# A rebuilt routing front, expert weights gathered with the token rows, and a half tile in another place

## The chip, the cores and the metric

One core of a Trainium2 chip runs the kernel. The metric is device time in microseconds (us) from the start to the end of one execution. PE is the matmul engine TensorE, DVE is VectorE, ACT is ScalarE, POOL is GpSimd, and SP is the engine that only issues transfers here.

## What is computed

A mixture of experts with a residual, over 4096 tokens of 256 numbers. Every token takes the two experts (of 8) with the largest gates, each expert is a three-layer network, and the results are added to the token, weighted by the gate's softmax.

```
gate = rms_w * (x * rsqrt(mean(x*x) + EPS)) @ wg_W + wg_b + (genre_embed @ gg_W + gg_b)
gate_w = softmax(gate);  topk_w, topk_i = top_k(gate_w, 2)
cw = sum(one_hot(topk_i, 8) * topk_w[..., None], axis=-2)
h1 = relu(x @ W1[e] + b1[e]);  h2 = relu(h1 @ W2[e] + b2[e]);  out_e = h2 @ W3[e] + b3[e]
x + sum over e of out_e * cw[e]
```

W1 is 256x512, W2 is 512x512 and W3 is 512x256 for each expert. Everything is float32.

## The kernel before, in words

**Tiles.** The 8192 (token, expert) pairs are sorted by expert into *slots*. A full tile is 256 slots (two halves of 128, `SUB` = 2) of one expert. What is left over of each expert goes into halves of its own: 71 halves (`MOST`) in all, so 36 tiles (`TILES`): 28 full ones, one more full one, four places (`PAIRS`) whose halves belong to different experts, and three more full ones. Three of the four places hold two halves each (*paired* tiles, steps 29 to 31), and the fourth holds one half only (the *half tile*). `TILE_AT` sets which tile stands at which step. In the kernel before the half tile is the last step, 35 (`LAST`), behind three full tiles.

**The front.** SP loads x in eight pieces and then copies x to `out` (eight transfers), since the results are added to `out` in memory. PE and DVE compute the gates, DVE picks the two experts of each token (`pick`), and PE counts them. DVE turns the counts into the order of the experts by size (`order`, signal `s_order`, for which SP waits before it loads the first weights) and into one slot number per (token, expert) pair. The slots are then inverted, from "slot of a token" to "token of a slot", by a sum of one-hot products: for each batch of 8 columns DVE makes `hot_r` (which row of a tile, 256 wide), `hot_c` (which tile, 36 wide) and `hot_q` (`hot_c` times three values: the token's number and its weight in two fp16 parts), and PE multiplies them, 16 matmuls a batch, eight batches. DVE reads the table of token numbers `tab_from` (signal `s_from`) out of the result, and later the tables `tab_to` and `tab_w` (signal `s_tab`). After batch 3 PE sums the squares of the first two experts' weights (`weight_sums`); ACT needs these to scale and split them (`weight_scales`, `high_parts`; `low_parts` on DVE), since each fp32 product is done as three fp16 ones.

On POOL, in this order: the softmax's sums, the weights' fp16 parts, the maximum over all partitions of the tokens' norms (`partition_all_reduce`), the scale of x (`s_sx`), the first expert's constants (`parameters(0)`), and only then the wait for `s_from` and the first gather.

**The steps.** For each tile i PE does `layer2(i)`, `layer1(i+1)`, `transpose_x(i+2)`, `layer3(i)`. ACT applies bias and relu (`activate`), DVE splits the result in two fp16 parts (`split`) and finishes the tile (`finish`), and ACT multiplies by the slots' weights (`weigh`, signal `s_y`). POOL's step i copies the tile's indices, gathers the rows of tile i+3 (two indirect transfers), does in steps 0, 3, 6, 9, 12, 15 and 18 (`PARAMETERS_AT`; step 0 and then each third one) the constants of one more expert, copies the constants of tile i+2 (`copy_parameters`, signal `s_prm`, for which ACT waits before it activates tile i+2's first layer), waits for `s_y` of tile i, copies the weights of tile i+2 (`cw`), and adds tile i's rows to `out` (two indirect transfers with an addition). Each engine runs its instructions in the order in which they are written, so a wait on POOL holds everything behind it. The half tile and the paired tiles have copies of their weights of their own, made by DVE (`copy_weights`).

Of the kernel before, what the change touches and what calls it, by code (L numbers as in the profile page):

```python
# [28 lines left out]
E = 8  # L29
# [12 lines left out]

MOST = (2 * N - E) // P + E
# [4 lines left out]
NAMES = FULL + 2 * PAIRS  # L48
RING = 3
# [7 lines left out]
WSCALE = float(2.0 ** 14)  # L57
# [4 lines left out]
RUNS = BATCH // RUN  # L62
# [17 lines left out]
LOWS_AT, SQUARES_AT, SUMS_AT, HIGHS_AT, PARAMETERS_AT = {0: 2, 1: 3}, {}, {}, {}, {0: 1}  # L80
# [8 lines left out]
assert max(LOWS_AT) < min(OWN_EARLY)  # L89
SUMS_BEHIND_BATCH = 3  # L90
OUT_PARTS = 8
WARM_START = 24
WARM_TILES = 96
# [11 lines left out]
def build_moe(nc, x, small_in, cond_in, weights, b3, out):  # L105
    with ExitStack() as ctx:
# [11 lines left out]
        area = sb("area", [P, J * H], F32)  # L118
# [3 lines left out]
        tab_w = sb("tab_w", [P, COLS], F32)  # L122
# [9 lines left out]
        iota_c = sb("iota_c", [P, TILES, RUN], F16)  # L132
# [25 lines left out]
        values = sb("values", [P, 3, 2 * J], F16)  # L158
# [23 lines left out]
        xg = take(RING * SUB * H).rearrange("p (s u h) -> p s u h", s=RING, u=SUB)  # L182
# [3 lines left out]
        assert at[0] == J * H  # L186
        x_sb = area[:, :].rearrange("p (j h) -> p j h", j=J)
# [7 lines left out]
        ex = take(E * J + J)  # L195
# [3 lines left out]
        floors, odd, odd_rank, half_at, later = (take(E) for _ in range(5))  # L199
        beyond = take(E * J)  # L200
        above, at_rank, weighed = (take(E * E).rearrange("p (a b) -> p a b", a=E) for _ in range(3))
# [3 lines left out]
        cand_ex = take(E * J + J)  # L205
# [4 lines left out]
        wt = take(2 * J)  # L210
        code, pad, pos_f, wsum = (take(COLS).rearrange("p (u t) -> p u t", u=SUB) for _ in range(4))
        tile16, row16 = (take(J).bitcast(F16) for _ in range(2))
        take(J)
        pairs = area[:, at[0]:at[0] + 2 * E * J]
        hot_c = take(BATCH * TILES).bitcast(F16).rearrange("p (r g c n) -> p r g c n", r=2, n=RUN, c=TILES)
        hot_r = take(BATCH * T).bitcast(F16).rearrange("p (r c n) -> p r c n", r=2, n=BATCH)
        hot_q = take(3 * BATCH * TILES).bitcast(F16).rearrange("p (r g v c n) -> p r g v c n", r=2, n=RUN, v=3, c=TILES)
        assert at[0] <= J * H

        def unread(first, n):  # L220
# [171 lines left out]
        def _(sp):  # L392
# [17 lines left out]
            for e in range(E):  # L410
# [11 lines left out]
                if e >= FRONT:  # L422
                    b3_rows(e)
# [876 lines left out]
```

## Time and profile before

| | us |
|---|---|
| median of 3 runs (lowest, highest) | 488.8 (487.81, 489.57) |
| the profiled execution's own time | 489.31 |
| its span, first to last instruction | 487.5 |
| first weights asked for by SP | 34.62 |
| `tab_from` written | 60.54 |
| first gather issued | 65.46 |
| `layer2(0)` begins | 79.01 |

The profiled execution took 1.8 us more than its span, and 0.5 us more than the median. Times in the rows are us from the span's start. PE is busy for 90% of the span, and the slices in which it is not are the first seven of forty and the last two.

### The profile page before, as it was taken

What the parts mean: (1) busy time and instruction counts of PE and PEld (TensorE: products, weight loads), DVE (VectorE), ACT (ScalarE), POOL (GpSimd) and SP (SyncE); (2) the same over time, 40 slices, a digit from 0 to 9 for tenths busy, and PEclk for the clock granted to TensorE, in tenths of its full rate; (3) what the DMA queues carried; (4) which work ended last, traced back from release to release, by engine and by line L of the source; (5) the groups of instructions that cost most, each with busy time, mean ns of one, the idle gap of its engine ahead of it and who ended that gap; (6) DMA issues with size and microseconds to landing.
All of it is one profiled execution on the core that took longest, in us unless ns stands there. A gap on an engine that the chain in (4) does not pass through costs nothing.

```text
span 487.5 us, 13260 instructions
## 1 busy us (share of the span) xinstructions
PE 438.4 (90%) x4330; PEld 393.0 (81%) x4330; DVE 312.7 (64%) x553; ACT 290.2 (60%) x607; POOL 295.8 (61%) x450
## 2 busy tenths in 40 slices
PE   6805969999999999999999999999999999999970
PEld 5504858898888888898898888888899899998860
DVE  3899753775676756657756756645556667775540
ACT  5706803767877778678678674545455555554530
POOL 5410175167777777777767777766666576565351
PEclk8955589999999999999999999999999999999996
DMA  8919416263363453332243431332232332002221
GB/s 285 393 39 364 168 45 227 85 156 55 116 155 66 110 152 67 113 49 41 45 64 120 64 57 24 55 66 46 38 52 46 52 47 46 24 24 46 26 33 19
DMA packets 18778, 44.85 MB, mean 92 GB/s; under 512 B 3963, under 2 KB 13245, under 8 KB 16541
## 3 DMA queue, kind: packets, MB, share of 16 engines
q0 software_dynamic: 13632, 17.71, 21.6%
q1 hardware_dynamic: 5008, 26.26, 14.8%
q8 instruction: 42, 0.69, 0.6%
q14 instruction: 19, 0.16, 0.1%
q10 hardware_dynamic: 77, 0.04, 0.0%
HBM read 35.60 MB, written 13.50 MB: 101 GB/s over the span
## 4 chain that ended last, share of the span: by engine, by line
PE 43%; POOL 19%; issue 14%; ACT 8%; DVE 7%; DMA 5%; POOLq 2%; DVEq 1%; SPq 0%; ACTq 0%
PE bank L1170 29%; PE bank L1204 7%; POOL out L575 6%; ACT area L721 3%; POOL area L554 2%; POOL bound L499 2%; DMA out<-area,cto 2%; DVE area L970 2%; ACT area L707 2%; ACT w_hi L675 2%; PE bank L1053 2%; ACT area L731 1%; PE bank L1126 1%; PE bank L1146 1%; DVE area L968 1%
## 5 line engine op out<-in xcount | busy, mean ns | idle before, releaser
L1170 PE MATMUL bank<-area,w_hi 128*128 128x256 f16 x1536 | 253.7, 273 | 3.4 <-DVE area L970 2.3
L1170 PE MATMUL bank<-area,w_lo 128*128 128x256 f16 x768 | 209.4, 273 | 0.0
L721 ACT ACTIVATE area<-bank,cprm 128x256 f32<-128x256 f32 (+1 forms) x264 | 132.4, 555 | 73.0 <-PE bank L1170 64.9
L1170 PEld LDWEIGHTS bank<-area,w_hi 128*128 x1536 | 149.7, 98 | 22.1 <-issue 4.9
L968 DVE CAST area<-area 128x512 f16<-128x512 f32 (+1 forms) x144 | 65.3, 453 | 131.2 <-ACT area L721 119.9
L575 POOL DMA_INDIRECT out<-area,cto x71 | 118.6, 1671 | 44.9 <-issue 26.3
L970 DVE TENSOR_TENSOR area<-area 128x512 f16<-128x512 f32 (+1 forms) x144 | 98.9, 687 | 5.0
L554 POOL DMA_INDIRECT area<-in_x,cfrom x65 | 69.5, 1070 | 38.5 <-POOL cfrom L549 27.9
L1204 PE MATMUL bank<-w_hi,area 128*128 x512 | 89.1, 273 | 1.0 <-DVE area L970 1.0
L1170 PEld LDWEIGHTS bank<-area,w_lo 128*128 x768 | 75.1, 98 | 8.7
L731 ACT ACTIVATE area<-area,cw 128x256 f32<-128x256 f32 x71 | 32.2, 499 | 74.2 <-DVE area L975 57.0
L1204 PE MATMUL bank<-w_lo,area 128*128 x256 | 69.8, 273 | 0.0
L1204 PEld LDWEIGHTS bank<-w_hi,area 128*128 128x128 f16 x512 | 50.1, 98 | 6.7 <-issue 1.2
L549 POOL COPY cto<-tab_to 128x2 int32<-128x2 int32 x36 | 33.9, 942 | 0.0
L549 POOL COPY cw<-tab_w 128x2 f32<-128x2 f32 x36 | 7.8, 218 | 41.0 <-ACT area L731 41.0
L695 ACT ACTIVATE area<-bank,small 128x512 f16<-128x512 f32 x36 | 24.9, 692 | 10.4 <-PE bank L1126 10.4
L549 POOL COPY cfrom<-tab_from 128x2 int32<-128x2 int32 x33 | 28.8, 874 | 0.0
L776 DVE SCALAR_TENSOR_TENSOR w_lo<-stage,scale,w_hi 128x1024 f16<-128x1024 f32 x20 | 24.8, 1277 | 4.6 <-POOL cprm L562 4.6
L957 DVE SCALAR_TENSOR_TENSOR area<-bank,small,area 128x512 f16<-128x512 f32 x36 | 26.8, 745 | 0.9 <-ACT area L695 0.9
L1204 PEld LDWEIGHTS bank<-w_lo,area 128*128 128x128 f16 x256 | 25.0, 98 | 2.9
L1126 PE MATMUL bank<-ident,area 128*128 128x128 f32 x142 | 22.1, 278 | 5.8 <-DMA area<-in_x,tab_from 4.8
L975 DVE SCALAR_TENSOR_TENSOR area<-bank,cprm 128x512 f32<-128x512 f32 x32 | 23.9, 746 | 4.8 <-PE bank L1204 3.9
(203 smaller groups left out, 486.5 us busy)
## 6 DMA issues: line engine op xcount, KB each, us to landing
stage<-in_weights SPq DMA_DIRECT2D x10, 1024.0 KB, 6.9
area<-in_x SPq DMA_DIRECT2D x8, 512.0 KB, 8.2
out<-in_x SPq DMA_DIRECT2D x8, 512.0 KB, 13.7
w_lo<-in_weights SPq DMA_DIRECT2D x4, 1024.0 KB
w_hi<-in_weights SPq DMA_DIRECT2D x2, 1024.0 KB, 9.9
out<-area,cto POOLq DMA_INDIRECT x71
area<-in_x,cfrom POOLq DMA_INDIRECT x65
prm<-in_b SPq DMA_DIRECT2D x8, 128.0 KB, 11.3
```

The lines of the kernel that those rows point to most:

```text
L549: pool.tensor_copy(to, table[:, bass.ds(i * SUB, SUB)]).then_inc(signal, 1)
L554: pool.indirect_dma_start(out=xg[:, s, u, :], out_offset=None, in_=x, in_offset=bass.IndirectOffsetOnAxis(ap=rows[:, u:u + 1].bitcast(U32) ...
L575: pool.indirect_dma_start(out=out, out_offset=bass.IndirectOffsetOnAxis(ap=cto[:, s, u:u + 1].bitcast(U32), axis=0), in_=yb[:, s, u, :], i ...
L695: act.activation(xt_hi, ps_x[:, :], ACT.Copy, scale=sx).then_inc(s_xhi, 1)
L721: ins = act.activation(to[:, m * T + u * wide:m * T + (u + 1) * wide], ps_h[layer][b][:, a * T + u * wide:a * T + (u + 1) * wide], ACT.Rel ...
L731: act.activation(yb[:, slot, u, :], y32[:, u * H:(u + 1) * H], ACT.Copy, scale=cw[:, slot, u:u + 1]).then_inc(s_y, 1)
L957: dve.scalar_tensor_tensor(xt_lo, ps_x[:, :], sx, xt_hi, ALU.mult, ALU.subtract).then_inc(s_xs, 1)
L968: dve.tensor_copy(hi_b, h_b).then_inc(half_done, 1)
L970: dve.tensor_tensor(lo_b, h_b, hi_b, ALU.subtract).then_inc(signal, 1)
L1126: ins = nc.tensor.transpose(ps_x[:, k * T + u * P:k * T + (u + 1) * P], xg[:, slot, u, k * P:(k + 1) * P], ident[:, :])
L1170: ins = nc.tensor.matmul(banks[m // 2][:, (m % 2) * T + u * wide:(m % 2) * T + (u + 1) * wide], weight, xp[:, cols], start=(k == 0 and n = ...
L1204: ins = nc.tensor.matmul(ps_y[:, u * H:(u + 1) * H], hp[:, cols], wp[:, bass.ds(w[u % len(w)] + (W3_AT + k * H), H)], start=(k == 0 and n ...
```

## The change

1. **Weights with the rows.** A new array in memory, `x_ext`, has for each token its 256 numbers and its 8 softmax weights (`ROW` = 264), with one spare row in the middle. SP fills the x part in the place where it copied x to `out` (rows of 1024 bytes at a pitch of 1056). POOL forms all 8 weights of each token (`dense`), and ACT issues two transfers that write them, 32 bytes to each row. The gathers read `x_ext` and wait for `s_ext`. `tab_w` is gone. POOL takes a tile's weights out of its gathered rows (`copy_weights` on POOL, behind the wait for `s_y`, with a register load of `order`).
2. **The copy of x to `out`** goes to SP's queue between the sixth and the seventh piece of weights, once the gather of tile 2 has landed. POOL waits for it (`s_out0`) before step 0, as it did before.
3. **A smaller inversion.** `hot_r` is 128 wide, `hot_c` has 72 columns and is multiplied by the token's number alone. All batches have buffers of their own. PE does 8 matmuls a batch. `tab_from` is one instruction from the result.
4. **Counts first.** The counts are summed over a partition before PE, the scan and the reciprocal run while PE counts, and instructions that don't depend on each other stand between those that do. `order` is written behind `upto` and `beyond`.
5. **The maximum over partitions** is a matmul by ones (`peaks`) in place of POOL's library function. The sums of the biases go to POOL, into its idle time.
6. **Second expert later.** ACT does `high_parts(1)` behind the second expert's squares, `(2)` behind `x_high(0)` and `(3)` in step 0. PE sums the second expert's squares behind the inversion; of the 96 warming matmuls 72 are left, 48 ahead of that sum and 24 behind it.
7. **The half tile** is step 32, directly behind the paired tiles. The last step is a full tile, whose third layer, finish, weighting and additions go by halves (`by_halves`, `layer3_parts`).

```diff
-AFTER = PAIRED_AT + PAIRS - 1
-LAST = TILES - 1
-TILE_AT = [*range(LEAST), *range(FULL - 1, LAST), *range(LEAST, FULL - 1), LAST]
+HALF_AT = PAIRED_AT + PAIRS - 1
+AFTER = HALF_AT + 1
+TILE_AT = [*range(LEAST), *range(FULL - 1, TILES), *range(LEAST, FULL - 1)]
-LOWS_AT, SQUARES_AT, SUMS_AT, HIGHS_AT, PARAMETERS_AT = {0: 2, 1: 3}, {}, {}, {}, {0: 1}
+LOWS_AT, SQUARES_AT, SUMS_AT, HIGHS_AT, PARAMETERS_AT = {0: 2, 1: 3}, {}, {}, {0: 3}, {0: 1}
...
+            sp.dma_start(x_ext[N // 2:N // 2 + 1, 0:H], x[0:1, :]).then_inc(s_ext, 16)
...
-            link(pool.partition_all_reduce(xmax_all, xmax, P, RED.max))
+            pool.tensor_tensor(je(dense), je(ex), over_e(rs), ALU.mult).then_inc(s_dense, 1)
+            pool.wait_ge(s_peak, 1)
...
+            def copy_weights(i, s, experts):
+                pool.wait_ge(s_xg[s], gathered(i) * 16)
+                for u, e in enumerate(experts):
+                    label = pool.value_load(order[0:1, bass.ds(e, 1)], min_val=0, max_val=E - 1)
+                    us = slice(u, u + 1) if paired(i) else slice(0, SUB)
+                    ins = pool.tensor_copy(cw[:, s, us].unsqueeze(2), xg[:, s, us, bass.ds(label + H, 1)])
+                ins.then_inc(s_cw, 1)
...
+            pool.wait_ge(s_ext, (OUT_PARTS + 4) * 16)
             pool.wait_ge(s_from, 1)
...
+            act.wait_ge(s_dense, 1)
+            for h in range(2):
+                first = h * (N // 2 + 1)
+                act.dma_start(x_ext[first:first + N // 2, H:ROW].rearrange("(p j) e -> p j e", j=J),
+                              je(dense)[h * P // 2:(h + 1) * P // 2]).then_inc(s_ext, 16)
...
-            inv = ps_slots.rearrange("p u (v t) -> p u v t", v=3)
-            link(dve.tensor_scalar(pos_f, inv[:, :, 0, :], 0.0, None, ALU.is_gt))
-            link(dve.scalar_tensor_tensor(code, inv[:, :, 0, :], float(N // 2), pos_f, ALU.add, ALU.subtract))
-            dve.tensor_copy(by_half(tab_from), code).then_inc(s_from, 1)
+            dve.wait_ge(s_inv, BATCHES)
+            dve.tensor_scalar(tab_from[:, :], ps_slots, float(N // 2), None, ALU.add).then_inc(s_from, 1)
```

**Place one, DVE's loop of the inversion.** Two batches of the kernel before. `iota_c` and `w_lo` hold the constants compared with, `values` the numbers multiplied in.

```order
L926 TENSOR_TENSOR area<-w_lo,area 128x2048 [waits s_spread,s_iota,s_dve]
L928 TENSOR_TENSOR area<-iota_c,area 128x288
L935 TENSOR_TENSOR area<-area,values 128x432 [waits s_wt,s_dve]
L935 TENSOR_TENSOR area<-area,values 128x432
L926 TENSOR_TENSOR area<-w_lo,area 128x2048
L928 TENSOR_TENSOR area<-iota_c,area 128x288
L935 TENSOR_TENSOR area<-area,values 128x432 [waits s_dve]
L935 TENSOR_TENSOR area<-area,values 128x432
L926 TENSOR_TENSOR area<-w_lo,area 128x2048 [waits s_inv]
```

Three batches of the kernel after; `w_hi` and `w_lo` are the buffers of their own.

```order
L985 TENSOR_TENSOR w_lo<-iota_c,area 128x1152 [waits s_spread,s_iota,s_dve]
L989 TENSOR_TENSOR w_hi<-w_lo,area 128x1024
L993 TENSOR_TENSOR w_lo<-w_lo,values 128x1152 [waits s_dve]
L989 TENSOR_TENSOR w_hi<-w_lo,area 128x1024
L985 TENSOR_TENSOR w_lo<-iota_c,area 128x1152
```

Four instructions for two batches stand in the place of eight, half as wide or less for each batch, and the wait for `s_inv` from the third batch on is gone.

**Place two, POOL's step 1.** Before, from the copy of the indices to the additions:

```order
L549 COPY cfrom<-tab_from 128x2 [waits s_xp]
L554 DMA area<-in_x,cfrom 128x256 [waits s_idx]
L554 DMA area<-in_x,cfrom 128x256
L561 TENSOR_LOAD etile
L561 ISA x2
L562 ISA
L562 COPY cprm<-prm 128x268
L549 COPY cw<-tab_w 128x2 [waits s_y,s_add]
L575 DMA out<-area,cto 4096x256 x2
```

After:

```order
L581 DMA area<-x_ext,cfrom 128x264
L589 TENSOR_LOAD etile
L589 ISA x2
L590 ISA
L590 COPY cprm<-prm 128x268
L599 ISA [waits s_y,s_add,s_xg0]
L599 TENSOR_LOAD order
L599 ISA x2
L601 ISA
L601 COPY cw<-area 128x2
L613 DMA out<-area,cto 4096x256 x2
```

Behind the wait for `s_y` there is now a register load and its arithmetic before the copy of the weights, and so before the two additions.

**Place three, SP's queue.** Before, from the load of x to the first weights, and then the seventh piece of weights:

```order
L397 DMA area<-in_x 128x1024 x7
L402 DMA out<-in_x 16x8192 x8
L411 TENSOR_LOAD order [waits s_order]
...
L417 ISA [waits s_low,s_xg1]
L417 DMA stage<-in_weights 128x2048
```

After, the same places:

```order
L415 DMA area<-in_x 128x1024 x7
L421 DMA x_ext<-in_x 512x256 x8
L422 DMA x_ext<-in_x 16x16
L423 DMA x_ext<-in_x 8x1
L432 TENSOR_LOAD order [waits s_order]
...
L438 DMA out<-in_x 16x8192 [waits s_xg2]
L438 DMA out<-in_x 16x8192 x7
L441 ISA [waits s_low]
L441 DMA stage<-in_weights 128x2048
```

The copy to `out` was in front of all weights; now one into `x_ext` in rows of 256 numbers is there, and the copy to `out` is behind the third tile's gather. The two transfers of ACT are `x_ext<-area 2048x1x8` in the same notation.

## Rows read from the trace of the kernel before

**Rows 1.** PE's waits from 80 to 450 us: engine, line, releaser, total, times, longest.
```profile
PE bank L1170 <- DVE area L970: 2.3, 5, 0.5
```

**Rows 2.** Busy time by stage: us, busy us of engines (x instructions), PE clock, DMA, GB/s.
```profile
30.00:40.00 10.00, 0.55 (x2) 0.00 (x0) 9.16 (x36) 0.97 (x2) 2.68 (x7) 0.50 0.43 164
...
60.00:70.00 10.00, 5.15 (x93) 5.01 (x90) 5.04 (x18) 1.13 (x2) 7.07 (x18) 0.99 0.09 27
```

**Rows 3.** Timeline of DVE in the front: start, us, line, operation [idle before <-releaser].
```profile
29.05 0.29 DVE L854 TENSOR_TENSOR area<-area 128x256 f16<-128x256 f16 x1
...
33.47 0.17 DVE L879 CAST order<-area 128x8 int32<-128x8 f32 x1
...
39.53 1.23 DVE L926 TENSOR_TENSOR area<-w_lo,area 128x2048 f16<-128x2048 f16 x1
40.67 0.30 DVE L928 TENSOR_TENSOR area<-iota_c,area 128x288 f16<-128x288 f16 x1
41.01 0.68 DVE L935 TENSOR_TENSOR area<-area,values 128x432 f16<-128x432 f16 x2
...
57.76 1.28 DVE L776 SCALAR_TENSOR_TENSOR w_lo<-stage,scale,w_hi 128x1024 f16<-128x1024 f32 x1
```

**Rows 4.** Timeline of ACT and of PE in the front.
```profile
41.90 1.06 ACT L656 ACTIVATE w_hi<-stage 128x1024 bf16<-128x1024 f32 x1 [0.41 <-DMA stage<-in_weights]
...
49.66 0.54 PE L1080 MATMUL bank<-small,ones 128*128 128x16 f32 x2
...
57.90 1.87 PE L1111 MATMUL bank<-area 128*128 128x108 f16 x16 [0.21 <-DVE area L935]
...
69.98 1.09 PE L1126 MATMUL bank<-ident,area 128*128 128x128 f32 x4 [4.85 <-DMA area<-in_x,tab_from]
```

**Rows 5.** Timeline of POOL and of SP's queue in the front.
```profile
47.38 0.46 POOL L538 PARTITION_ALL_REDUCE small<-small  x1 [10.23 <-issue]
57.26 0.39 POOL L539 TENSOR_SCALAR small<-small 128x1 f32<-128x1 f32 x1 [9.41 <-issue]
...
60.82 0.30 POOL L499 TENSOR_SCALAR bound<-fsq,small 128x1 f32<-128x1 f32 x1 [1.29 <-issue]
...
65.46 1.30 POOL L554 DMA_INDIRECT area<-in_x,tab_from  x1 [0.57 <-POOL prm L516]
...
73.71 0.95 POOL L554 DMA_INDIRECT area<-in_x,tab_from  x1 [0.30 <-issue]
...
34.62 1.99 SPq L417 DMA_DIRECT2D stage<-in_weights  x3
```

**Rows 6.** The chain that ended last, steps 0 and 1: start, us, what.
```profile
79.01 8.03 PE bank L1170 x72
...
90.09 7.86 PE bank L1170 x72
```

**Rows 7.** DMA queues in four windows (1.75:2, 78.5:79, 118:118.5, 16:24): packets, MB, share.
```profile
q1 hardware_dynamic: 10, 0.04, 104.4%
q10 hardware_dynamic: 52, 0.03, 42.3%
...
q1 hardware_dynamic: 16, 0.13, 66.7%
q0 software_dynamic: 15, 0.06, 29.8%
...
q0 software_dynamic: 58, 0.06, 86.7%
...
q1 hardware_dynamic: 184, 3.02, 103.7%
```

**Rows 8.** Timeline of POOL, step 3 with the constants of an expert.
```profile
114.79 0.18 POOL L549 COPY cw<-tab_w 128x2 f32<-128x2 f32 x1 [0.43 <-ACT area L731]
...
130.15 0.81 POOL L562 COPY cprm<-prm 128x268 f32 x1 [0.73 <-POOL prm L516]
```

**Rows 9.** Timeline of POOL at the end.
```profile
478.86 1.55 POOL L575 DMA_INDIRECT out<-area,cto  x1 [3.13 <-DMA out<-area,cto]
```

More of the change, by code:

```diff
@@ L198, in build_moe @@
         cmp_h = take((2 * PAIRS + 1) * E)
-        floors, odd, odd_rank, half_at, later = (take(E) for _ in range(5))
+        floors, odd, odd_rank, half_at, later, base = (take(E) for _ in range(6))
+        rowtot = take(E // 2).bitcast(F16)
         beyond = take(E * J)
-        above, at_rank, weighed = (take(E * E).rearrange("p (a b) -> p a b", a=E) for _ in range(3))
+        above, at_rank, weighed, below = (take(E * E).rearrange("p (a b) -> p a b", a=E) for _ in range(4))
         key, rank_of, order_f = (take(E) for _ in range(3))
@@ L262, in halves_of, with halves_before @@
         def halves_of(i):
-            return MOST - SUB * i if i == LAST else SUB
+            return MOST - SUB * (TILES - 1) if i == HALF_AT else SUB
+        def halves_before(i):
+            return sum(halves_of(n) for n in range(i))
         def two(i):
@@ L289, in rows, with gathered @@
             return ap.rearrange("p (e j) -> p e j", e=E)
-        def by_half(table):
-            return table[:, :].rearrange("p (t u) -> p u t", u=SUB)
+        def gathered(i):
+            return sum(halves_of(n) for n in range(i % RING, i + 1, RING))
         def over_j(ap):
@@ L413, in _ @@
                     if q == PLACES:
-                        sp.wait_ge(s_xg[1], SUB * 16)
+                        sp.wait_ge(s_xg[2], SUB * 16)
+                        for n in range(OUT_PARTS):
+                            rows = slice(n * N // OUT_PARTS, (n + 1) * N // OUT_PARTS)
+                            sp.dma_start(out[rows, :], x[rows, :]).then_inc(s_out0, 16)
                     if BEFORE[q] is not None:
@@ L886, in _ @@
-            link(dve.tensor_reduce(half_at, weighed, AX.X, ALU.add))
-            link(dve.tensor_scalar(half_at, half_at, -1.0, float(MOST * P), ALU.mult, ALU.add))
-            link(dve.tensor_tensor(later, half_at, rows_end, ALU.subtract))
+            link(dve.tensor_tensor(rows(sel16), ej(oh1), ej(oh2), ALU.add))
+            with nc.allow_low_precision(reason="counts up to J are whole numbers"):
+                dve.tensor_reduce(rowtot, rows(sel16), AX.X, ALU.add).then_inc(s_sel, 1)
+            dve.tensor_tensor_scan(running, restart[:, :], sel16, 0.0, ALU.mult, ALU.add)
@@ L999, in step @@
                 split(i, 1)
-                if next1 and two(i) and two(i + 1):
+                if next1 and two(i) and paired(i + 1):
                     copy_weights(i + 1, 0, 1)
@@ L1007, in step @@
                     x_low(i + 2)
-                if next2 and i + 2 > PAIRED_AT and two(i + 2):
-                    for u in range(SUB):
+                if next2 and i + 2 > PAIRED_AT and paired(i + 2):
+                    for u in range(halves_of(i + 2)):
                         copy_weights(i + 2, u, 0)
@@ L1234, in layer3_last, with step @@
                             ins.then_inc(s_l3, 1)
-            def step(i, s, turn, sums=None, next1=True, next2=True):
+            def step(i, s, sums=None, next1=True, next2=True):
                 w = weights_at(i)
```

357 lines of the change are left out of this document (192 added, 165 removed).

## The prediction, made before the changed kernel was run

> **What bounds the kernel now.** I read the busy times by stage first, then the timelines of the five engines up to the first steps, then PE's waits, then the DMA queues. There are three regimes. From step 0 on PE sets the pace: between 80 and 450 us its only waits of note are five of at most 0.5 us, 2.3 us together [rows 1]. The end costs a few us more. The front is the reserve: PE is busy for 0.55 of the ten us from 30 on, at a granted clock of 0.50 [rows 2].
>
> In the front two chains run to the first gather at 65.46 us. One is DVE's: the picks until 29.05, `order` at 33.47, the slots until 39.53, the loop of the inversion until 57.76, PE's last batch until 57.90 + 1.87 = 59.77 [rows 3, 4], and `tab_from` behind it. The other is POOL's. It stands before its library function for 10.23 us and behind it for 9.41, and is free only at 57.26. The constants of the first expert begin at 60.82, and the gather follows them at 65.46 [rows 5]. So the gather is issued some 5 us later than the table would allow. From the gather to `layer2(0)` at 79.01 it is 13.55 us [rows 5, 6].
>
> **The change part by part.** Against the profiled execution's 489.3 us.
>
> *Slots.* Six instructions' worth of waiting between dependent ones goes, an addition goes, and the reciprocal runs while PE counts; one reduction, one strided addition and one maximum from PSUM come, some 0.3 us each. I take the last slot at 37.8 in place of 39.5, and `order` about 1 us later (34.6), since two wide instructions now stand in front of it. So the weights land 1 us later too. Bounds: 0.5 to 2.5 us gained.
>
> *Loop.* A 2048-wide comparison takes 40.67 - 39.53 = 1.14 us to the next start, a 432-wide product 0.30 (two of them 0.68 with their latency) [rows 3]. By width, 1024 columns are 0.60 and 1152 are 0.67. A pair of batches is 2 x 0.67 + 2 x 0.60 = 2.55, four pairs are 10.2, and the loop ends at 48.0 (before 57.76). PE needs 1.87 / 16 = 0.117 us a matmul at the low clock [rows 4], 0.94 a batch, and keeps up until batch 3. There it stands before the first expert's sums. The squares of its second piece begin at 41.90 and take 2.3 [rows 4]; 1 us later they end at 45.2. The sums are three matmuls like the one of 0.54 at 49.66 [rows 4], pipelined about 1.4, so 46.6, and the last 32 matmuls 3.8: 50.4. `tab_from` is one instruction behind: 50.7, in place of 60.5.
>
> *POOL.* Without the library function POOL waits for ACT's scales, at 47.5. The constants took 65.46 - 60.82 = 4.64 with the gap in front of the gather [rows 5]: first gather at 52.3, in place of 65.46, if `x_ext` is full. That is 13.2 us sooner, and POOL is now behind the table by 1.6 only.
>
> *Gather to step 0.* Alone it would repeat. But the six pieces of weights still move until about 56, and beside such a piece POOL's and SP's queues shared a half us with 15 and 16 packets [rows 7]; I add 1.5 us to the first landing. PE gets a clock of 1.00 for the transposes and saves 0.5, and DVE, ACT have their other pieces done. `layer2(0)` begins at 66.2, which is 12.8 us sooner. Bounds: 10 to 15.
>
> *Is `x_ext` full at 52.3?* The x part, in 4096 rows, follows x on the queue; the copy it replaces moved 3.02 MB in 8 us [rows 7]. An add row, which reads and writes memory, is the dearest row of that size: 58 packets in 0.867 x 16 x 0.5 us, 0.12 us each [rows 7]. x itself is as large as the copy and goes first, until about 13.7. So the 4096 rows take between 11 and 31 us on 16 DMA engines and end between 25 and 45. I take 16 us, ready by 30, nearer the plain copy. The weights' part is 4096 pieces of 32 bytes. The reciprocal ends by 31.2, POOL's product takes 0.8 and ACT's issue and the start of a transfer 1.8: from 33.8 on. Small packets of the ACT queue went at 52 in 0.25 us beside SP's 4 KB ones, on 11 of the 16 DMA engines [rows 7]; at that rate 4096 take about 14 us, and end at 47.5. Hidden by 5 us. This is the thin cover of the whole change.
>
> *The copy to `out`.* Its gate is the third gather, whose last half was issued 73.71 - 65.46 = 8.25 us behind the first and lands some 2.7 later: 63.3. At 3.02 MB in 8 us [rows 7] the 4.19 MB take 11.1, with issue and landing 13.5: 76.8. POOL waits there with step 0 behind it. Then come the gather of tile 3 (3.6 us), the constants of the second expert (3.9) and the copy for tile 2 (1.2): 85.5. ACT wants that copy when `layer1(2)` ends: a step of 11.0 and 72 matmuls of 7.9, less a little, behind `layer2(0)` [rows 6]. That is 18.6, at 84.8, and what follows on ACT and DVE takes as long as PE has other work. I take a stall of 1.6 us; bounds 0 and 4 (POOL's lateness carried into step 3).
>
> *The register load on POOL.* In a step with constants the chain runs from `s_y` at 114.79 through POOL's additions, gather and constants to `cprm` at 130.15 + 0.81, and ACT, DVE and PE follow [rows 8]: these are the steps in which PE waits 0.5 us [rows 1]. So POOL's path has no slack there, six times. The nearest price of a load with its arithmetic is the gap of 0.73 before `cprm` [rows 8], less 0.1 for the handover that is there anyhow: 0.65 each, 3.9 us. Bounds: 0, if hidden, and 8, if the 1056-byte rows also make a gather's issue as dear as an addition's (1.55 for about 1.0).
>
> *The end.* The half tile's steps on PE are too short to cover the latency of activation and split behind `layer1`: about 1 us each at the two steps around it. At the end two rows of additions instead of one follow a longer last layer, but `layer1(35)` covers what cost 1.05 before. The last addition no longer stands 3.13 us for the one before [rows 9], since the one before is older by then. I count +0.6; bounds -1 and +2.5.
>
> *Sum.* -12.8 + 1.6 + 3.9 + 0.6 = -6.7: 482.6 for an execution like the profiled one, which is 0.5 above the median. I say 482.
>
> **The rivals.**
> 1. *Turn by turn.* If the DMA engines take one packet of ACT's queue and one of SP's in turn, as the 15 beside 16 packets look like [rows 7], the 32-byte pieces crawl beside 8 KB ones. Each DMA engine has 256 of them. Some 75 go before the weights start, 52 beside as many large packets in 17 us, and the other 130 take 5 us: full at 59.5. The gather is 7.2 us late and saves the 1.5 of contention: 488. Against it: the 52 small packets beside 10 large ones, in the same rows. The Trainium skill's page "DMA: Bandwidth & Descriptors", section "Queues, rings and completion order", says that an engine drains a whole packet of typically 9 to 17 descriptors from a ring before it switches; by that rule the pieces would pass in groups and this rival would not arise. The trace has nothing of 32 bytes to show it.
> 2. *Dear pieces: slower than before.* If each 32-byte piece costs what an add row costs, 0.12 us [rows 7], 256 of them take 30.6 us: full at 64.4, the gather 12.1 late less 1.5, in sum +3.9 against before: 492.7. It decides against the change once `x_ext` is full later than about 62. For it: no transfer here writes so little to memory; against it: an add row moves 32 times as much, both ways. The same page's table "Specifications" puts 512 bytes as the least for full rate, with a read-modify-write below; by that rule this rival is nearer than by the small loads of the rows, which no run here shows yet.
> 3. *POOL becomes the bound of the steps.* Its loads and dearer gathers at their upper bound (+4) and the stall at 4 (+2.4): 488.5.
> 4. *The POOL terms are hidden.* No stall, no price: 476.6. Against it: the chain through the constants, in which nothing hides [rows 8].
>
> **How the numbers follow.** Forecast 0.55 (478 to 486); rival 1 0.14; rival 2 0.07; rival 3 0.12; rival 4 0.12. The range takes rivals 1, 3 and 4 in: 477 to 490. A measurement here can tell 0.3%, 1.5 us. Faster by more (below 487.3): the forecast, rival 4 and the near parts of 1 and 3: 0.76. Within: 0.11. Slower: 0.13. The forecast's own range is 478 to 486.
>
> **What would show it.** `tab_from` near 50.7, the first gather near 52.3, `layer2(0)` near 66; if the first gather waits for a DMA, it is rival 1 or 2, and the landing tells which. POOL's step 0 begins near 77 and PE waits once in step 1 or 2. In the steps with constants PE's waits grow from 0.5 to 1.1 us. PE waits around the half tile. The forecast fails if small writes are slow, or if POOL had slack that the chain does not show.

## The result, and the profile after

The changed kernel takes 490.19 us (median of 20 runs, 489.14 to 493.20) where before takes 488.01 on the same chip (20 runs): a ratio of 1.0063, 95% interval 1.0045 to 1.0081. The ratio is that of the means (490.77 and 487.68), 3.1 us; the medians are 2.2 us apart. Either way the changed kernel is slower; the forecast was 482, and faster. The profiled execution spans 490.2 us. It is one of the longer ones, 493.0 us by its own time, and a second profile of the same kernel (experiment 11) spans 486.7.

The front came as forecast or better. The first gather is at 53.67 (forecast 52.3; before 65.46, [rows 5]) and `layer2(0)` at 68.24 (forecast 66.2; before 79.01, [rows 6]). What went wrong is behind it. POOL's timeline of the changed kernel, from the last gather of the front to the first additions:

```profile
61.01 1.96 POOL L581 DMA_INDIRECT area<-x_ext,tab_from  x1 [0.31 <-DMA area<-x_ext,tab_from]
62.98 0.30 POOL L601 COPY cw<-area 128x2 f32 x2
80.06 0.35 POOL L576 COPY cto<-tab_to 128x2 int32<-128x2 int32 x1 [16.78 <-DMA out<-in_x]
80.36 1.25 POOL L576 COPY cfrom<-tab_from 128x2 int32<-128x2 int32 x1
82.40 0.97 POOL L581 DMA_INDIRECT area<-x_ext,cfrom  x1 [0.79 <-POOL cfrom L576]
83.67 0.94 POOL L581 DMA_INDIRECT area<-x_ext,cfrom  x1 [0.30 <-issue]
...
90.19 0.40 POOL L590 COPY cprm<-prm 128x268 f32 x1 [0.74 <-POOL prm L534]
...
91.93 1.73 POOL L613 DMA_INDIRECT out<-area,cto  x1 [0.67 <-issue]
93.96 1.56 POOL L613 DMA_INDIRECT out<-area,cto  x1 [0.30 <-issue]
```

POOL stands idle 16.78 us for the copy of x to `out`, which nothing needs before the additions at 91.93. ACT's timeline of the same stretch shows what follows: the output of tile 0 is weighed (L779) at 82.32, so its additions come some 9 us behind it, and then ACT itself stands for tile 2's constants.

```profile
82.32 0.91 ACT L779 ACTIVATE area<-area,cw 128x256 f32<-128x256 f32 x2
...
90.63 1.93 ACT L769 ACTIVATE area<-bank,cprm 128x256 f32<-128x256 f32 x4 [4.31 <-POOL cprm L590]
```

PE's timeline, and its waits from 80 to 450 us (total, times, longest). Before they were 2.3 us behind DVE [rows 1] and, which the prediction did not count, 0.9 us for gathered rows:

```profile
PE bank L1126 <- DMA area<-in_x,cfrom: 0.9, 2, 0.8
```

Now six waits for gathered rows, 8.6 us, come first:

```profile
90.64 0.66 PE L1174 MATMUL bank<-ident,area 128*128 128x128 f32 x4 [3.45 <-DMA area<-x_ext,cfrom]
```

```profile
PE bank L1174 <- DMA area<-x_ext,cfrom: 8.6, 6, 3.5
PE bank L1218 <- DVE area L1022: 4.8, 8, 1.4
```

Behind the pause the granted clock is lower for a while (busy us of PE, PEld, DVE, ACT, POOL, then the clock):

```profile
80.00:90.00 10.00, 7.19 (x66) 6.19 (x64) 4.74 (x7) 5.00 (x10) 7.20 (x18) 1.00 0.86 313
90.00:100.00 10.00, 9.36 (x70) 7.73 (x71) 6.31 (x9) 6.51 (x13) 7.19 (x8) 0.83 0.40 73
```

A clean mark to split the time is the transposes of tile 2, the first PE work that no kernel here waits for. Before, they begin at

```profile
86.87 0.49 PE L1126 MATMUL bank<-ident,area 128*128 128x128 f32 x3
```

and 487.5 - 86.87 = 400.6 us follow. In the changed kernel they begin at

```profile
76.11 0.60 PE L1174 MATMUL bank<-ident,area 128*128 128x128 f32 x4
```

10.8 us sooner, and 490.2 - 76.11 = 414.1 us follow: 13.5 us are given back. By the transposes of later tiles, the lead over before falls from 10.76 us at tile 2 to 7.15 at tile 3 and 5.43 at tile 4; then by 4.7 us in small pieces until tile 29, and by 3.4 from there to the end. In the second profile of the changed kernel the same four stretches lose 6.1, 1.6, 2.5 and 1.3 us, 11.6 in all.

The end of the changed kernel, on PE: around the half tile, waits of 1.28, 1.39 and 0.57 us.

```profile
437.48 2.85 PE L1218 MATMUL bank<-area,stage 128*128 128x128 f16 x48 [1.28 <-DVE area L1022]
...
446.63 0.39 PE L1218 MATMUL bank<-area,w_hi 128*128 128x256 f16 x2 [1.39 <-DVE area L1022]
458.28 0.39 PE L1218 MATMUL bank<-area,w_hi 128*128 128x256 f16 x2 [0.57 <-DVE area L1022]
```

### The profile page after: what moved, and what is told of

Its sections match the earlier page's. It is cut to its first block, busy times and chain, and to the rows that moved or that the text cites. A ratio compares the mean times of both kernels' runs of the same rounds, so it can differ in the third digit from the quotient of the medians.

```text
span 490.2 us, 13276 instructions
## 1 busy us (share of the span) xinstructions
PE 432.0 (88%) x4244; PEld 383.9 (78%) x4244; DVE 307.8 (63%) x531; ACT 290.0 (59%) x608; POOL 305.7 (62%) x456
## 4 chain that ended last, share of the span: by engine, by line
POOL 28%; PE 27%; issue 13%; DMA 7%; DVE 7%; ACT 6%; POOLq 4%; SPq 1%; DVEq 1%; another core or an unknown queue 0%; ACTq 0%
PE bank L1218 19%; POOL out L613 12%; PE bank L1252 6%; POOL area L581 5%; DMA area<-x_ext,cfrom 3%; POOL bound L517 2%; ACT area L755 2%; DMA out<-in_x 2%; POOL cfrom L576 2%; POOLq L599 2%; DVE area L1022 2%; DMA stage<-in_weights 1%; POOL cto L576 1%; DVE stage L1046 1%; DVE area L1020 1%
## 5 line engine op out<-in xcount | busy, mean ns | idle before, releaser
L1020 DVE CAST area<-area 128x512 f16<-128x512 f32 (+1 forms) x144 | 67.1, 466 | 140.0 <-ACT area L769 127.5
L581 POOL DMA_INDIRECT area<-x_ext,cfrom x65 | 69.5, 1069 | 37.7 <-POOL cfrom L576 27.9
L1252 PE MATMUL bank<-w_hi,area 128*128 x496 | 87.9, 276 | 0.0
L779 ACT ACTIVATE area<-area,cw 128x256 f32<-128x256 f32 x71 | 32.3, 500 | 71.5 <-DVE area L1027 53.0
L1252 PE MATMUL bank<-w_lo,area 128*128 x248 | 68.4, 276 | 0.0
L1252 PEld LDWEIGHTS bank<-w_hi,area 128*128 128x128 f16 x496 | 49.0, 99 | 6.1 <-issue 0.2
L1174 PE MATMUL bank<-ident,area 128*128 128x128 f32 x142 | 22.3, 280 | 11.8 <-DMA area<-x_ext,cfrom 8.6
L576 POOL COPY cfrom<-tab_from 128x2 int32<-128x2 int32 x33 | 30.1, 912 | 0.0
L601 POOL COPY cw<-area 128x2 f32 (+1 forms) x39 | 11.0, 286 | 28.7 <-ACT area L779 21.3
L1174 PEld LDWEIGHTS bank<-ident,area 128*128 128x128 f32 x142 | 16.4, 143 | 14.0 <-DMA area<-x_ext,cfrom 10.3
```

What stands on the lines that cost most here:

```text
L576: pool.tensor_copy(to, table[:, bass.ds(i * SUB, SUB)]).then_inc(signal, 1)
L581: pool.indirect_dma_start(out=xg[:, s, u, :], out_offset=None, in_=x_ext, in_offset=bass.IndirectOffsetOnAxis(ap=rows[:, u:u + 1].bitcast( ...
L779: act.activation(yb[:, slot, u, :], y32[:, u * H:(u + 1) * H], ACT.Copy, scale=cw[:, slot, u:u + 1]).then_inc(s_y, 1)
L1020: dve.tensor_copy(hi_b, h_b).then_inc(half_done, 1)
L1174: ins = nc.tensor.transpose(ps_x[:, k * T + u * P:k * T + (u + 1) * P], xg[:, slot, u, k * P:(k + 1) * P], ident[:, :])
L1252: ins = nc.tensor.matmul(ps_y[:, u * H:(u + 1) * H], hp[:, cols], wp[:, bass.ds(w[u % len(w)] + (W3_AT + k * H), H)], start=(k == 0 and n ...
```

## Experiments

All are timed beside before on the same chip. Gains in us are differences of two ratios times 488; each has an interval of some 1.3 to 2.4 us to either side, and in experiment 5 the ratio of the medians (0.9808) is 0.2% off the ratio given. "Behind" is the span less the start of tile 2's transposes in the kernel's own profile, to be held against 414.1 (changed) and 400.6 (before).

### 1. The wait for the copy to `out`

```diff
-            pool.wait_ge(s_out0, OUT_PARTS * 16)
             for i in range(TILES):
...
+                if first:
+                    pool.wait_ge(s_out0, OUT_PARTS * 16)
                 if not first:
                     pool.wait_ge(s_add, halves_before(i) * 16)
```

> Edit: in the changed kernel POOL waits for the copy of x to out only right before the additions of tile 0, and no longer before step 0; nothing else moves. The ledger of the changed kernel against before is: transposes of tile 2 10.76 us sooner; 3.61 of it lost until tile 3's, whose gather POOL issued at 82.4 only after standing 16.78 us for that copy; 1.72 more until tile 4's, in the stretch where the granted clock is 0.83. Theory A (the position of the wait makes the stall): the gather of tile 3, the constants of the second expert and tile 2's copies all stand before 75, PE's wait of 3.45 us goes, the clock stays 1.00, and 4 to 5.3 us come back: 485 to 486.2 where the changed kernel has 490.2. Rival B (the transfers are late because the queue is full of weights and the copy, whoever issues them): tile 3's rows land near 88 anyhow, and the time stays within 1.5 us. Rival C (POOL's lateness is what the later steps run on: once it is on time, the waits of 0.4 to 1.5 us for gathers in steps 4 to 20 go too): 7 to 9 us, 481 to 483.

Measured: ratio 0.9897 (0.9864 to 0.9931). Against 1.0063 that is 1.7%, 8.1 us (some 1.8 to either side) for one moved line; behind 405.0. The number is theory C's, its mechanism is not. POOL's timeline shows its work of step 0 done early, and POOL ahead of ACT in that step:

```profile
62.48 0.17 POOL L576 COPY cto<-tab_to 128x2 int32<-128x2 int32 x1
...
70.82 0.40 POOL L590 COPY cprm<-prm 128x268 f32 x1 [0.73 <-POOL prm L534]
83.43 0.43 POOL L601 COPY cw<-area 128x2 f32 x1 [12.21 <-ACT area L780]
```

Tile 3's transposes do not wait at all, and the clock stays at 1.00 from 80 to 100. But theory C wanted the later waits for rows to go as well, and they stay, at tiles 7, 10 and 22 (0.98, 1.10 and 1.38 us; in the second profile of the changed kernel 0.86, 0.96 and 1.37). PE's waits for rows from 80 to 450 us in this kernel:

```profile
PE bank L1175 <- DMA area<-x_ext,cfrom: 3.7, 4, 1.4
```

What moved is the stretch from tile 2's transposes to tile 4's: 22.6 us here, 27.5 and 30.0 in the two profiles of the changed kernel. From tile 4 to tile 29 it is 282.2 here and 284.2 and 282.0 there. So 5.0 to 7.4 us are the stall with what follows it directly, and against the second profile nothing is left for later tiles.

### 2. The register load

```diff
-                    label = pool.value_load(order[0:1, bass.ds(e, 1)], ...)
-                    ins = pool.tensor_copy(cw[...], xg[:, s, us, bass.ds(label + H, 1)])
+                    ins = pool.tensor_copy(cw[...], xg[:, s, us, H:H + 1])
```

> Edit: the weights' copy on POOL takes a fixed column of the gathered rows (the column of expert label 0) in place of the one that a register load names; so the outputs are weighted with the wrong gate, and everything else is as in the changed kernel. It prices the register load alone. In the changed kernel the tiles 4 to 22 lose 4.7 us against before. Theory A (POOL's chain from one tile's output through additions, gather and constants is what PE waits for in the steps with constants, and the load adds 0.45 to 0.65 us to it once or twice): the waits of PE for gathers in steps 4 to 20 fall from 5.2 us to about 1 and the time by 3 to 4.7 us, 485.5 to 487.2. Rival B (the gathers are late since rows of 1056 bytes out of the copy take longer to issue or land than rows of x): under 1 us, 489.2 to 490.2.

Measured: 0.9963 (0.9941 to 0.9986), 1.0% or 4.9 us under the changed kernel, with some 1.4 us of uncertainty; behind 408.2. Theory A. From tile 4 to tile 29 it takes 279.9 us, nearly as before the change (279.4). That longer rows are not what costs is in the groups of POOL's instructions of the changed kernel (xcount | busy us, mean ns): a gather takes 1069 ns, and 1070 in the same view of before.

```profile
L581 POOL DMA_INDIRECT area<-x_ext,cfrom x65 | 69.5, 1069 | 37.7 <-POOL cfrom L576 27.9 <-issue 9.7
```

### 3. The half tile

The tables of order, names and tests of before are put back into the changed kernel, so that the half tile is step 35 (`HALF_AT = TILES - 1`).

> Edit: in the changed kernel the half tile goes back to the last place, with its own weights copied as before and the last full tile added whole; the front and the gathered weights stay. The transposes of tile 29 stand 0.70 us sooner than before in the changed kernel, and the span ends 2.7 us later: 3.4 us are lost from there on. Theory A (the order does it: PE's waits of 1.28, 1.39, 0.57 and 0.56 us around the half tile and the longer last layer cost more than the chain of additions that they replace): 3.0 to 3.8 us come back, 486.4 to 487.2. Rival B (the last addition's landing or POOL's work by halves sets the end either way, and the waits around the half tile have their like at the end): within 1 us, 489.2 to 491.

Measured: 1.0009 (0.9989 to 1.0029), 2.6 us under the changed kernel; behind 410.1. Theory A, a little smaller.

### 4. Gathers one step sooner

```diff
+            pool.wait_ge(s_xp, 1)
+            copy_columns(cfrom[:, 0, :], tab_from, 3, s_idx)
+            gather(3, 0, cfrom[:, 0, :])
             pool.wait_ge(s_out0, OUT_PARTS * 16)
...
-                    pool.wait_ge(s_xp, i + 1)
-                    gather(i + 3, s, cfrom[:, s, :])
+                    pool.wait_ge(s_xp, i + 2)
+                    gather(i + 4, s1, cfrom[:, s1, :])
```

> Edit: POOL issues each gather one step sooner: tile 3's behind the first three, before the wait for the copy to out, and tile i + 4's in step i; the slot it writes is free by then. The constants and their copies stay where they are. Theory A (latency: only the gathers are late): all six waits of PE for gathered rows go, 8.6 us; in their place the copies of constants set the steps with constants, at some 0.5 us each as before, and tile 2's copy behind the copy to out still costs 3 to 4: 484.5 to 487. Rival B (throughput: POOL has more to do in three steps, 34.9 us between 104.55 and 139.50, than PE with 33.8, so whatever is taken off one thing it is late with the next): POOL's lateness moves to the copies of constants and the additions, within 1.5 us of the changed kernel, 488.7 to 490.2.

Measured: 0.9935 (0.9913 to 0.9957), 6.2 us under the changed kernel, a little more than theory A's 3.2 to 5.7; behind 407.3. It is theory A in that no wait for rows is left, and from tile 4 to 29 it takes 277.0 us, 2.4 less than before the change. The stall is not gone: the constants of tile 2 hold PE up in their place, for longer, and the clock falls further:

```profile
92.99 0.60 PE L1224 MATMUL bank<-area,w_hi 128*128 128x256 f16 x2 [4.96 <-DVE area L1028]
```

```profile
90.00:100.00 10.00, 7.01 (x42) 5.24 (x43) 6.68 (x10) 6.00 (x12) 7.71 (x8) 0.66 0.53 127
```

### 5. Three things at once

The moved wait, the half tile last, and the register load made ahead of the wait for a tile's output:

```diff
-                    experts.append(e)
+                    experts.append(pool.value_load(order[0:1, bass.ds(e, 1)], ...))
                 ins.then_inc(s_prm, 1)
```

> Edit: the changed kernel with three things taken out of POOL's and PE's way at once: the wait for the copy to out stands right before tile 0's additions, the register load that names the weights' column is made beside the parameters' one and not behind the wait for a tile's output, and the half tile is last again. The front and the gathered weights stay, so this is the front alone. Theory A (the three losses are apart and there are no others): by the ledger the front gave 10.8 us in the changed kernel's profile and 11 to 13 in the profiles of the others, and nothing is lost behind it: 11 to 13 us faster than before, ratio 0.973 to 0.978, 474 to 477 beside 487 of before. Rival B (one and the same lateness of POOL was counted several times): the stall's removal alone gave 8.1 us of which the ledger gave it 5.3, so the sum of the single gains, 8.1 + 4.9 + 2.6, overlaps by 3 to 5 us: ratio 0.979 to 0.984, 477 to 479.5.

Measured: 0.9830 (0.9795 to 0.9865), 477 to 479.5 as rival B has it; behind 401.9. The three single gains add to 15.6 us, together they are 11.4, a difference of 4.2 with some 3.3 to either side. Rival B's reason, one lateness counted twice, is not shown by it. Experiment 2 took the register load out; here it is only made earlier, so part of its price may stay (from tile 4 to 29 it takes 280.8 us, and 279.9 without the load, which is not more than two executions of one kernel differ by).

### 6. The same with gathers one step sooner

> Edit: the kernel of the three changes, and POOL issues each gather one step sooner. Theory A (latency of the gathers is what is left of POOL's chain): PE waits for no gathered rows at all, the waits for constants in the steps with constants stay at 0.3 to 0.5 us each, and it gains 1 to 3 us over the kernel of the three changes, ratio 0.970 to 0.976. Rival B (with POOL on time the gathers have slack already): under 1 us between the two.

Measured: 0.9761 (0.9728 to 0.9794), 3.4 us under experiment 5 (some 2.3 to either side), a little over theory A's 1 to 3; behind 398.4. PE's list has no wait for rows any more.

### 7. And the constants in another order

```diff
-                if late is not None:
-                    link(parameters(late))
                 if next2:
                     experts = copy_parameters(i + 2, s2)
+                if late is not None:
+                    link(parameters(late))
```

> Edit: the kernel with all of it, and in a step with constants POOL copies the constants of tile i + 2 before it makes those of the next expert, which that copy does not need. Theory A (the copies of constants are 5 us late six times, and PE's waits of 0.3 to 0.5 us for DVE behind them are their price): the six waits go and 1.5 to 2.5 us with them, against the kernel without the swap. Rival B (these waits hang on PE's sums of the squares or on the order on ACT, not on POOL): within 0.5 us.

Measured: 0.9694 (0.9663 to 0.9726), 471.7 us, 3.3 us under experiment 6 (some 2.2 to either side), a little over theory A's 1.5 to 2.5; behind 395.8. Theory A by its mechanism; the waits in the steps with constants are gone, and a wait of 1.1 us at `layer2(0)` heads what is left:

```profile
PE bank L1227 <- DVE area L1029: 1.1, 1, 1.1
PE bank L1261 <- DVE area L1029: 1.0, 1, 1.0
```

### 8. The swap alone

> Edit: the changed kernel with the swap alone (the copy of constants for tile i + 2 before the constants of the next expert are made); wait for the copy to out, register load, half tile and gathers are as in the changed kernel. In step 0 the copy for tile 2 comes at 85 in place of 90.2, but tile 3's gather lands at 90.6 as before. Theory A (in the stall and in the steps with constants the gather is the last to come, and the constants next to it): the stall stays, PE's waits for gathered rows stay at 8 to 9 us, the waits behind DVE go, and the gain is 1 to 3 us: 487 to 489. Rival B (the copy for tile 2 is what stalls the changed kernel): the stall of step 1 halves and the gain is over 4 us: below 486.

Measured: 1.0065 (1.0035 to 1.0095), nothing against the changed kernel; behind 414.6. Both theories expected a gain. PE's waits behind DVE did shrink, to 2.9 us from 80 to 450, but those for gathered rows grew to 11.4, four times (8.6 and 9.2 in the two profiles of the changed kernel): what POOL did sooner in one place it did later in another.

```profile
PE bank L1174 <- DMA area<-x_ext,cfrom: 11.4, 4, 5.0
PE bank L1218 <- DVE area L1022: 2.9, 2, 1.6
```

### 9. Weights held back behind tile 3's rows

```diff
                             sp.dma_start(out[rows, :], x[rows, :]).then_inc(s_out0, 16)
+                        sp.wait_ge(s_xg[0], 2 * SUB * 16)
```

> Edit: the changed kernel with the swap (which alone moved nothing: 1.0065 beside 1.0063), and SP issues the weights that follow the copy to out only when tile 3's gathered rows have landed. The wait for the copy to out stays before step 0. It splits the stall in step 1 into its two halves: POOL's late issue (80.06 for the wait, gather issued at 82.4) and the landing (7 us behind the last issue, with 2 to 3 MB of weights on the queue at 90 to 100% of the DMA engines' time). Theory A (the landing among the weights is most of it): the rows land 3 us behind their issue, near 86 to 87, PE waits 0 to 2 us in place of 5.0, and with the lost clock and what later steps inherit, 4 to 6 us come back: ratio 0.994 to 0.998. Rival B (the issue is too late in any case, or the held weights stall the squares in the next steps): under 2 us, ratio over 1.002.

Measured: 1.0042 (1.0016 to 1.0067), 1 us under the changed kernel, not told from nothing; behind 413.5. By the number rival B, by the mechanism neither. The landing did depend on the weights: tile 3's rows, issued at 81.95 and 83.23, were there at 86.58 and held PE up for 0.93 us in place of 5.00 in experiment 8. But the stall moved one tile on. PE's timeline at tiles 3 and 4:

```profile
86.58 0.66 PE L1175 MATMUL bank<-ident,area 128*128 128x128 f32 x4 [0.93 <-DMA area<-x_ext,cfrom]
...
103.92 1.11 PE L1175 MATMUL bank<-ident,area 128*128 128x128 f32 x4 [5.84 <-DMA area<-x_ext,cfrom]
```

and POOL's, where the gather of tile 4 can only follow the additions of tile 0, and these the constants of the second expert:

```profile
80.85 0.19 POOL L577 COPY cto<-tab_to 128x2 int32<-128x2 int32 x1 [17.91 <-DMA out<-in_x]
...
94.34 1.80 POOL L614 DMA_INDIRECT out<-area,cto  x1 [0.67 <-issue]
...
99.21 1.03 POOL L582 DMA_INDIRECT area<-x_ext,cfrom  x1 [0.86 <-POOL cfrom L577]
```

So it is POOL's lateness in steps 0 and 1 that counts, not one transfer. PE pays for it once, wherever the pause falls: from tile 2's transposes to tile 4's it takes 29.3 us here and 29.1 in experiment 8.

### 10. The half tile behind the pairs, with POOL on time

> Edit: the fastest kernel so far (wait for the copy to out before the additions, early register load, gathers one step sooner, the copy of constants before the next expert's constants) with the half tile back behind the paired tiles, as the change has it. It prices the place of the half tile where POOL is on time. Theory A (the place itself costs): from the transposes of tile 29 to the end it took 100.2 and 100.5 us in the profiles with the half tile behind the pairs and POOL nearer to time, and 98.4 to 98.9 with it last: 1.5 to 2 us slower than the kernel with it last, ratio 0.973 to 0.974. Rival B (its price of 2.6 us in the changed kernel is the place's in full, whatever POOL does): ratio 0.975 to 0.977. Rival C (on time there is no price): 0.969 to 0.971.

Measured: 0.9719 (0.9688 to 0.9750), 1.2 us over experiment 7, which ran on another chip and whose interval overlaps with it: between A and C, undecided. Behind 397.0 against 395.8. The waits around the half tile are still there, 1.27 and 0.65 us.

### 11. The changed kernel again

> Edit: none; the changed kernel again, on the same chip as the two beside it and later than its first timing. Both theories expect the ratio to before of the first timing, 1.0063 with an interval of 0.0018 to either side; the profile shows how far the marks of one kernel move between two executions: the start of layer 2 of tile 0 (68.24 in the first profile, 66.0 to 67.7 in those of the variants with the same front), the wait of 3.45 us for tile 3's rows, and the stretch from tile 29 to the end (102.4 there, 100.2 to 100.5 in the variants).

Measured: 1.0056 (1.0030 to 1.0082). Its profile has `layer2(0)` at 66.61, tile 3's rows 5.98 us late, 100.3 us from tile 29 to the end, and 412.2 behind. So single marks move by 1 to 2.5 us between executions of one kernel, and the 3.4 us that the first profile gave to the end were 1 to 2 too many.

### 12. POOL's steps in the kernel before

> Edit: the kernel before (its front, its table of weights, its half tile last) with POOL's steps as in the fastest variant: each gather one step sooner, the wait for the copy to out behind step 0's work, and the copy of constants before the next expert's constants. It says how much of the fastest variant's 0.9694 is the front's. Before, PE waits 3.2 us in steps 4 to 20 for rows and for DVE behind constants (0.47, 0.18, 0.45, 0.46, 0.46, 0.43, 0.75), and the wait for the copy to out costs nothing (POOL stands 10.58 us for ACT in step 0). Theory A (the gains add up: front 10.8 to 13 us, POOL's steps 3.2): ratio 0.993 to 0.995, and the front's share of the fastest variant is the rest, 11 to 12 us. Rival B (POOL's steps were worth more, as the swap's gain of 3.7 us on the kernel with all of it hints, whose own waits for DVE were 2.3): ratio 0.988 to 0.991.

Measured: 0.9887 (0.9850 to 0.9924), 5.5 us under before; behind 396.2, which is 4.4 less than before. Rival B. Against experiment 7 it leaves 0.9694 / 0.9887 = 0.9805 for all the rest of the change, 9.5 us. Its profile also shows that the front of before is not always as late as in [rows 5]: with the same front, the first gather was at 61.52 in place of 65.46. Most of that, 2.6 us, is there at the end of work that all these kernels share. DVE's last copy of the gates, in before, in this kernel and in the changed one:

```profile
21.89 0.29 DVE L808 COPY w_lo<-bank 128x128 f32<-128x128 f32 x1 [0.55 <-PE bank L1064]
```

```profile
19.25 0.29 DVE L815 COPY w_lo<-bank 128x128 f32<-128x128 f32 x1 [0.55 <-PE bank L1071]
```

```profile
19.60 0.29 DVE L848 COPY w_lo<-bank 128x128 f32<-128x128 f32 x1 [0.55 <-PE bank L1112]
```

## Why the prediction was wrong

**The step that failed is "the copy to `out`".** It took a stall of 1.6 us, at most 4; taking the stall away is worth 8.1. Its own chain gave less still, 85.5 against 84.8, and the text does not say how that 0.7 becomes 1.6. Three things in it were short. Step 0 began at 80.06, not 76.8. Tile 3's rows, in the prediction's chain there some 2.7 us behind their issue and so in time, landed 6 us behind the end of their last issue, since SP sends the next weights right behind the copy, as experiment 9 shows; and it is these rows that stop PE first, not tile 2's constants. In the changed kernel's SP queue:

```profile
64.84 5.22 SPq L438 DMA_DIRECT2D out<-in_x  x8
70.26 1.03 SPq L441 DMA_DIRECT2D stage<-in_weights  x2
```

And a pause costs more than itself: some 1.8 us of lower clock follow it, which the prediction did not count.

The profiles, split at the transposes of tiles 2, 4 and 29, put each loss in its own stretch (us):

| profile | tile 2 to 4 | 4 to 29 | 29 to the end |
|---|---|---|---|
| before | 22.2 | 279.4 | 99.0 |
| changed, first and second | 27.5, 30.0 | 284.2, 282.0 | 102.4, 100.3 |
| 1, wait moved | 22.6 | 282.2 | 100.2 |
| 2, no register load | 28.0 | 279.9 | 100.3 |
| 3, half tile last | 28.3 | 282.6 | 99.2 |
| 4, gathers sooner | 29.8 | 277.0 | 100.5 |
| 5, three at once | 22.2 | 280.8 | 98.9 |
| 7, all | 22.2 | 274.9 | 98.7 |
| 12, before with POOL's steps | 22.3 | 275.0 | 98.9 |

All seven profiles with the wait at the head of step 0 and the new front (experiments 8 and 9 too) have 27.5 to 30.0 us in the first stretch, the five with it moved have 22.2 or 22.6. The middle stretch shows no dependence on where this wait stands. What moves it is the register load (experiment 2) and the moment at which gathers are issued (experiment 4). Before, POOL had slack in the steps: it waited for ACT's outputs 21 times, 41.0 us together, in the line of its copies of weights (10.6 of it in step 0). With the register load a plain step of POOL (9.6 us from 94.96 to 104.55 in the changed kernel) is only 1.3 us shorter than one of PE (10.92), while a step with constants is over 4 us longer (15.3). So POOL comes late behind a set of constants, and PE waits 0.4 to 1.5 us for the next rows. It is not that POOL has too much work: with the same work and the gathers one step sooner the stretch takes 277.0 us. And it comes late after an early start as after a late one: the last gather for tile 7 is issued 4.3 us before that tile's transposes in experiment 1 and in the changed kernel alike. I read this so that an early start can't be saved up: POOL then stands 12.21 us for the output of tile 0. This part is the prediction's term "The register load on POOL".

**Slots, loop, POOL without the library function.** Right as mechanisms: the loop takes 10.2 us (36.57 to 46.8, as forecast), `tab_from` is at 48.26 (50.7), the first gather at 53.67 (52.3), behind POOL's constants. Counted from the gates, though, the slots gained less than the text gave them: 36.57 - 19.60 = 17.0 us in place of 39.53 - 21.89 = 17.6, 0.7 and not 1.7, and `order` came 2.2 us later and not 1.

**Gather to step 0.** -12.8 was forecast for `layer2(0)`, and -10.8 to -13.0 is what the profiles with the new front show against the one of before. But that one profile of before had a late start: its gates were ready 2.3 us later than the changed kernel's, in work that both share. By tile 2's transposes the new front has 73.9 to 76.1 in its twelve profiles, 74.7 on average, the old one 86.87 and 81.55: 7 to 12 us. Measured in time, 9.5 us by experiments 7 and 12, with some 2.4 to either side (on two chips, and with the price of the gathered weights still in it). The term was right as a mechanism and, made against one execution, some 3 us too large.

**Is `x_ext` full?** Right that it is hidden, and by far more than 5 us. The DMA queues of the changed kernel from 32 to 34 us: packets, MB, share of 16 engines.

```profile
q10 hardware_dynamic: 3314, 0.11, 76.3%
```

That is 0.763 x 16 x 2 us / 3314 = 0.0074 us for a piece of 32 bytes. The 4096 pieces had passed by 36, rivals 1 and 2 (full at 59.5 and 64.4) did not come, and the first gather waited for POOL's own constants. The Trainium skill's "DMA: Bandwidth & Descriptors", section "Specifications", has transfers under 512 bytes pay a read-modify-write; no price of it shows in this trace.

**The register load.** 3.9 was forecast with bounds 0 and 8; 4.9 was measured, and by the mechanism named: no slack in the chain through the constants. In the profile without the load 2.1 us of it (against the second profile; 4.3 against the first) are from tile 4 to 29, and 2.0 in the stretch of the stall, where two executions of the changed kernel differ by 2.4 themselves. Gathers of longer rows cost nothing more.

**The end.** +0.6 was forecast, at most 2.5; 2.6 was measured in the changed kernel (interval of some 1.4 to either side), and 1.2, not told from zero, where POOL is on time. The two waits around the half tile were in the text; that `layer1(35)` makes up for them was not so.

**The sum.** -9.5 for the front and, behind tile 2's transposes, 11.6 and 13.5 lost (412.2 and 414.1 against 400.6) make +2.1 to +4.0, and +3.1 was measured (0.63% of 488). By single terms it is -9.5 + 8.1 + 4.9 + 2.6 = +6.1; with the 11.4 that the last three have together, +1.9. Each of these has its 1.3 to 2.4 us of uncertainty. So against the forecast of -6.7 the stall is the largest error (+6.5), the front the next (+3.3), and the end and the register load add 2.0 and 1.0. The rival nearest in number is "POOL becomes the bound of the steps" (488.5, chance 0.12). Of its parts, the loads came at 4.9 and not near 8, dearer gathers did not come, and the stall went past its upper bound of 4; no rival had a stall of this size.

## What to carry to other kernels

When a front is made shorter, look at each engine's wait for something slow that used to be hidden by it: the copy to `out` was free before, moved later by the change while the steps moved earlier, and a wait placed at the head of a loop made all of POOL's first step late. Follow the late engine to everything that it issues, the rows of the next tile too, and add to a pause what the lower clock costs behind it. Do not take later waits for consequences of an early stall until a profile without the stall shows them gone: here they stayed, and had a cause of their own. And when removing one wait gains nothing (experiments 8 and 9), look whether the same lateness shows up one tile on before calling it off: the same swap was worth 3.3 us once POOL was on time.

## What was not expected of the hardware

- Small writes: 0.0074 us of a DMA engine each for pieces of 32 bytes, 16 times less than the 0.12 us of an addition's row [rows 7].
- A pause of 3.5 to 6 us of PE has a price beyond itself, and it hardly depends on the pause's length. In five profiles (the changed kernel twice, experiments 2, 3 and 8) PE waited 3.45, 5.98, 4.00, 4.27 and 5.00 us for tile 3's rows, and from tile 2's to tile 4's transposes they took 1.8 to 1.9 us more than the wait and the 22.2 us without a stall. Behind the 3.45 us the mean granted clock over ten us was 0.83 (0.66 behind the 4.96 of experiment 4, and 1.00 without a pause). Of the third-layer matmuls in the changed kernel's first profile three began in each 0.64 us from 91.90 to 94.46, the lower of the two levels (1.2 GHz), and three in 0.32 us from 94.99:

```profile
91.90 0.63 PE L1252 MATMUL bank<-w_hi,area 128*128 x2
...
94.99 0.38 PE L1252 MATMUL bank<-w_hi,area 128*128 x2
```

- The first 20 us are not the same in every execution: with the same code the gates were ready at 21.89 in one and at 19.25 in another, and the runs of before beside experiment 5 lie between 484.1 and 489.4 us.
- In the changed kernel's first profile POOL waited 4.98 us for an addition near the half tile to land, and PE 1.39 us behind it; in experiment 1 it was 3.27 and 0.65. The second profile of the same kernel has 3.25 and 0.65, so this belongs to the execution and not to the kernel. What made the landing late there stays open.
